# A gated cross-attention and quantised feed-forward block on one core: work at the edges of its stages rearranged

## What is computed

```python
x = x + tanh(g_xattn) * attention(layernorm(x), ctx)   # x: 4 x 512 x 1024, ctx: 4 x 64 x 1024
x = x + tanh(g_ffn)   * ffn(layernorm(x))

# attention: 32 query heads and 8 key/value heads of 128, rotary angles, causal mask
queries, keys, values = rope(h @ Wq.T), rope(ctx @ Wk.T), ctx @ Wv.T
attn = softmax(where(causal, queries @ keys.T * 128**-0.5, min))   # 64 keys
out = (attn @ values) @ Wd.T

# ffn, 1024 -> 512 -> 1024, rows and weights rounded to whole numbers up to 127
gate, up = quant(h * inv_gate) @ w_gate.T, quant(h * inv_up) @ w_up.T   # scaled back
inter = clip(silu(gate) * up, -10, 10)
out = quant(inter * inv_inter) @ w_down.T
```

## Time and profile before

| | |
|---|---|
| median of three executions | 1485.55 us |
| the profiled execution | 1490.73 us |
| its span, first to last instruction | 1488.9 us |
| TensorE, VectorE, ScalarE, GpSimd busy | 1431.8, 1005.5, 563.2, 614.7 us |
| mean granted clock of TensorE | 0.993 |
| key and value stage, up to the first queries | about 64 us |
| half 0, half 1 of the attention | to about 711 us, to about 1351 us |
| feed-forward loop | about 1351 us to the end |

### The profile page before, as it was taken

The page is one execution under the profiler, slowest core; times in us unless marked ns, Lnnn a source line. Parts: engine busy times, 40 slices in busy tenths (PEclk is TensorE's granted clock), DMA queues, the critical chain, the costliest instruction groups (busy, mean ns, idle before and its releaser), DMA issues.

```text
span 1488.9 us, 19163 instructions
## 1 busy us (share of the span) xinstructions
PE 1431.8 (96%) x7248; PEld 1169.9 (79%) x7248; DVE 1005.5 (68%) x1563; ACT 563.2 (38%) x864; POOL 614.7 (41%) x429
## 2 busy tenths in 40 slices
PE   7999999999999999999999999999999999997887
PEld 7878888888888888887878888888888888874443
DVE  5866575757576766667475757566666666677997
ACT  4424141414242323244542423232322323147995
POOL 3435242434343343440343433434433434233784
PEclk9999999999999999999999999999999999998999
DMA  8834343433425243437265242433333334464565
GB/s 296 251 95 107 72 114 72 106 88 82 112 64 119 68 106 80 108 78 238 74 177 137 70 107 61 95 76 94 83 89 86 94 72 108 93 206 148 120 128 99
DMA packets 327131, 166.52 MB, mean 112 GB/s; under 512 B 275200, under 2 KB 290048, under 8 KB 326656
## 3 DMA queue, kind: packets, MB, share of 16 engines
q1 hardware_dynamic: 324448, 154.29, 39.0%
q0 software_dynamic: 2592, 11.01, 4.5%
HBM read 132.74 MB, written 35.65 MB: 113 GB/s over the span
## 4 chain that ended last, share of the span: by engine, by line
PE 79%; DVE 12%; ACT 3%; DMA 2%; issue 2%; POOL 2%; SPq 1%; ACTq 0%; POOLq 0%; DVEq 0%
PE psum L561 16%; PE psum L563 16%; PE psum L562 16%; PE psum L615 8%; PE psum L650 7%; PE psum L652 7%; PE psum L651 7%; DVE psum L1625 2%; DVE vw_lo L1354 1%; DVE res L1672 1%; DMA acc<-in_x 1%; DMA wv_raw<-in_wv_t 1%; DVE xg L1635 1%; POOL rot L1239 1%; DVE pt_lo L1354 1%
## 5 line engine op out<-in xcount | busy, mean ns | idle before, releaser
L561 PE MATMUL psum<-xt_hi,wq_hi 128*128 128x512 f32 x1024 | 402.1, 393 | 2.6 <-DVE xt_lo L1354 2.6
L562 PE MATMUL psum<-xt_lo,wq_hi 128*128 128x512 f32 x1024 | 399.7, 390 | 0.0
L563 PE MATMUL psum<-xt_hi,wq_lo 128*128 128x512 f32 x1024 | 399.7, 390 | 0.0
L1211 POOL TENSOR_TENSOR wq_lo<-wq_raw,wq_hi 128x512 fp32r<-128x512 f32 x128 | 170.0, 1340 | 490.7 <-ACT wq_hi L918 490.7
L1515 DVE TENSOR_TENSOR acc<-psum,acc 128x512 f32<-128x512 f32 x224 | 151.3, 681 | 140.3 <-PE psum L652 140.3
L1239 POOL TENSOR_TENSOR rot<-rot 128x1024 f32<-128x1024 f32 x64 | 153.5, 2399 | 207.8 <-DVE rot L1458 207.0
L561 PEld LDWEIGHTS psum<-xt_hi,wq_hi 128*128 128x128 f32 x1024 | 193.1, 189 | 42.2 <-DVE xt_lo L1354 2.8
L563 PEld LDWEIGHTS psum<-xt_hi,wq_lo 128*128 128x128 f32 x1024 | 192.9, 188 | 40.8
L964 ACT ACTIVATE vw_hi<-psum 64x512 fp32r<-64x512 f32 x256 | 151.4, 591 | 194.0 <-PE psum L563 190.3
L562 PEld LDWEIGHTS psum<-xt_lo,wq_hi 128*128 128x128 f32 x1024 | 192.9, 188 | 39.5
L1354 DVE TENSOR_TENSOR vw_lo<-psum,vw_hi 64x512 fp32r<-64x512 f32 x256 | 175.4, 686 | 52.9 <-ACT vw_hi L964 46.8
(11 more groups left out here) (151 smaller groups left out, 1915.8 us busy)
## 6 DMA issues: line engine op xcount, KB each, us to landing
wq_raw<-in_wq_t SPq DMA_DIRECT2D x128, 256.0 KB, 4.4
wd_raw<-in_wd_t SPq DMA_DIRECT2D x128, 256.0 KB, 3.6
p_scratch<-prob SPq DMA_DIRECT2D x60, 256.0 KB, 2.0
pt_raw<-p_scratch SPq DMA_DIRECT2D x240, 64.0 KB, 2.5
acc<-in_x SPq DMA_DIRECT2D x16, 512.0 KB, 5.5
out_x<-acc SPq DMA_DIRECT2D x16, 512.0 KB, 3.9
xa<-out_x SPq DMA_DIRECT2D x16, 512.0 KB, 3.6
out_x<-res POOLq DMA_DIRECT2D x15, 512.0 KB, 5.5
```

The lines of the kernel that those rows point to most:

```text
L561: pe.matmul(dst, a_hi, b_hi, start=start, stop=False)
L562: pe.matmul(dst, a_hi, b_lo, start=False, stop=False)
L563: return pe.matmul(dst, a_lo, b_hi, start=False, stop=stop)
L1211: pool.tensor_tensor(dst, full, hi.bitcast(F32), ALU.subtract).then_inc(done, 1)
```

## The change

**The start.** The statistics of tiles 6 and 7 move from VectorE to ScalarE (`late_statistics`: a Copy with a running sum, then a Square with one, and two small scalings). On VectorE the low parts of rows 2 and 3 move ahead of the statistics of tile 5, and `key_rows(7)` moves ahead of the normalisation of tiles 4 to 7. TensorE transposes tile 4 one query part later (half 0 only).

**The first group of each half.** `values(gg, 2)` moves from between parts 6 and 7 of unit 2 to behind part 1 of unit 3, with its copies on ScalarE and VectorE.

**The end of each half.** The subtraction of the softmax (`softmax_less`) moves behind `add(2)`, and its last multiplication (`softmax_c`) behind `add(3)`. Elsewhere the two new functions directly follow the steps that they are cut from.

**The feed-forward loop.** The root of tiles 8 to 11 is taken at step 2 and that of tiles 12 to 15 at step 8 (before: one root for 8 to 15, at step 4). The four `deviations` of tiles 12 to 15, two at step 2 and two at step 3 before, come one each at steps 4 to 7. The scaling of `v_sd` moves from ScalarE to GpSimd, ahead of its loop.

```diff
 # tensor, slot(): first group
-                    else:
+                    elif half:
                         turn_rows(half, 4)
                     queries(unit, 4)
                     if not filled:
+                        if half == 0:
+                            turn_rows(half, 4)
                         turn_rows(half, 5)
...
                     queries(unit, 6)
-                    values(gg, 1 if filled else 2)
+                    if filled:
+                        values(gg, 1)
                     queries(unit, 7)
                 if kind == 3 and not filled:
-                    for part in range(1, 4):
-                        queries(unit, part)
+                    queries(unit, 1)
+                    values(gg, 2)
+                    queries(unit, 2)
+                    queries(unit, 3)
 # scalar
+            def late_statistics():
+                last, junk = slice(HTILES - 2, HTILES), bank(O_BANK, 2)
+                act.wait_ge(xt_lo_done, 2)
+                for t in (HTILES - 2, HTILES - 1):
+                    act.wait_ge(x_in[t], 16)
+                    if t == HTILES - 1:
+                        act.wait_ge(late_done, 1)
+                    act.activation(junk, acc[:, t, :], ACT.Copy, accum_out=mv[:, t, 0:1]).then_inc(late_done, 1)
+                act.wait_ge(late_done, 2)
+                act.activation(mv[:, last, 0], mv[:, last, 0], ACT.Copy, scale=1.0 / DIM).then_inc(late_done, 1)
+                for t in (HTILES - 2, HTILES - 1):
+                    act.wait_ge(late_done, 3 + t - HTILES + 2)
+                    act.activation(junk, acc[:, t, :], ACT.Square, scale=-1.0, bias=mv[:, t, 0:1], accum_out=mv[:, t, 1:2]).then_inc(late_done, 1)
+                act.wait_ge(late_done, 5)
+                act.activation(mv[:, last, 1], mv[:, last, 1], ACT.Copy, scale=1.0 / DIM).then_inc(stat_done, 2)
...
-                if n == HTILES:
-                    act.wait_ge(norm2_done, 2)
+                if n in (HTILES, HTILES + BT):
+                    act.wait_ge(norm2_done, n // BT)
...
             copy_rows(0, 3)
+            late_statistics()
             root(HTILES, slice(BT, HTILES))
...
                 if s == 2:
-                    down_columns()
-                if s < 4:
-                    deviations(1, 2 * s)
-                    deviations(1, 2 * s + 1)
-                if s == 4:
-                    root(TILES + 2, slice(HTILES, TILES))
+                    root(TILES + 2, slice(HTILES, HTILES + BT))
+                if BT <= s < HTILES:
+                    deviations(1, s)
+                if s == HTILES:
+                    root(TILES + 3, slice(HTILES + BT, TILES))
 # gpsimd
             pool.wait_ge(fv_in, 32)
+            pool.tensor_scalar(v_sd[:, :], v_sd[:, :], gates[:, 1:2], 1.0, ALU.mult, ALU.mult).then_inc(vd_done, 1)
 # vector, last_outputs()
                 softmax_a(unit - 1)
                 add(gg - 1, 2)
+                softmax_less(unit - 1)
                 softmax_b(unit - 1)
                 add(gg - 1, 3)
+                softmax_c(unit - 1)
 # vector, the loop of the feed-forward
-                if s == 4:
-                    variances(slice(HTILES, TILES), TILES)
-                if s == 5:
-                    second_norm(5, 1)
+                if s == 1:
+                    variances(slice(HTILES, HTILES + BT), HTILES + BT)
+                if s == 3:
+                    second_norm(5, slice(HTILES, HTILES + BT))
+                if s == HTILES:
+                    variances(slice(HTILES + BT, TILES), TILES)
+                if s == HTILES + 1:
+                    second_norm(6, slice(HTILES + BT, TILES))
```

More of the change, by code:

```diff
@@ L1423, in reciprocal_root, with second_norm @@
                 dve.wait_ge(small_done, small)
-            def second_norm(n, half):
-                tiles = slice(half * HTILES, (half + 1) * HTILES)
+            def second_norm(n, tiles):
                 reciprocal_root(n, tiles, rstd2)
@@ L1469, in softmax_a, with softmax_less @@
                 dve.tensor_reduce(red[:, 0, :], view, AX_X, ALU.max).then_inc(max_done, 1)
+            def softmax_less(unit):
+                view = scores.rearrange("p (s k) -> p s k", k=KEYS)
                 dve.wait_ge(max_done, unit + 1)
@@ L1485, in softmax_b, with softmax_c @@
                 dve.tensor_scalar(top[:, 2, :], top[:, 2, :], gates[:, 0:1], None, ALU.mult).then_inc(share_done, 1)
+            def softmax_c(unit):
+                top = rows_of_softmax(unit)
                 dve.wait_ge(share_done, unit + 1)
@@ L1591, in slot @@
                         lower_probs(unit - 2)
-                    else:
-                        lower_values(gg, 2)
                 if kind == 3 and not filled:
                     turn_second(unit - 1)
+                    lower_values(gg, 2)
                     softmax_a(unit - 1)
+                    softmax_less(unit - 1)
                     lower_probs(unit - 2)
@@ L1620, in slot @@
                 if half == 1 and u == UPG + 1:
-                    second_norm(4, 0)
+                    second_norm(4, slice(0, HTILES))
             def greatest(top, src, done):
@@ L1782, in _ @@
             row_statistics(4)
+            lower_rows(0, 2)
+            lower_rows(0, 3)
             row_statistics(5)
             key_rows(6)
-            lower_rows(0, 2)
-            lower_rows(0, 3)
-            row_statistics(6)
-            row_statistics(7)
-            aggregate(slice(BT, HTILES), HTILES)
-            reciprocal_root(2, slice(BT, HTILES), rstd1)
-            normalise(4)
-            normalise(5)
-            normalise(6)
-            normalise(7)
-            key_rows(7)
+            key_rows(7)
+            aggregate(slice(BT, HTILES - 2), HTILES - 2)
+            reciprocal_root(2, slice(BT, HTILES), rstd1)
+            for t in range(BT, HTILES):
+                normalise(t)
             dve.wait_ge(cst_in, 32)
```

14 lines of the change are left out of this document (6 added, 8 removed).

## The result

The changed kernel takes 1491.06 us in the median of 20 executions (1486.85 to 1493.03), the kernel before 1486.53 (20 executions beside it, 1483.41 to 1490.83). The ratio is 1.0028, 95% interval 1.002 to 1.0036: slower by 4.2 us (3.0 to 5.4; 4.5 by the two medians), where 6.5 faster was forecast. The profiled executions hide most of it: 1491.20 us after with a span of 1489.4, 1490.73 before with 1488.9.

What follows compares the result with a forecast made beforehand. TensorE was taken to bound the attention, VectorE the feed-forward loop. Start -2.2, value block -3.7 and -2.0, additions +1.05 and loop +0.4 gave -6.45, from the median 1485.55 to 1479.1 us; range 1474.5 to 1482.0.

Steps and rivals of the forecast that it cites:

- What bounds the kernel: In both attention halves TensorE runs back to back, so a wait removed there is time gained one for one.
- The start, forecast -2.2: Start: queries begin without the 2.6 us wait and 1.5 us fall; a new 1.65 us wait for tile 4; gain 2.2 us.
- The four tiles take 2.98 us, to 72.6: Start: VectorE's normalisations of tiles 4 to 7 keep their earlier length of 2.98 us and end at 72.6.
- normalisation starts 67.9 + 1.86 - 0.2: Start: keys of block 7 done at 67.9, shorter aggregation after them, so VectorE's first normalisation starts at 69.55.
- The value block, forecast -3.7 and -2.0: First group of each half: value stall of 2.09 us goes; half 0 gains 3.7 us including a clock fall, half 1 2.0.
- The limit in half 1: Value block, half 1: GpSimd's query turn behind the wq roundings holds the score to 757.9; gain 2.0 of a possible 2.7.
- The additions, forecast +1.05: End of each half: the multiplication delays the sixth output 0.65 us, half 1's fifth output is 0.4 late; 1.05 us slower.
- The loop, forecast +0.4: Feed-forward loop: next step 1.0 us earlier, then steps 4 to 9 take 47.95 against 46.53; net 0.4 us slower.
- The next step starts 2.2 - 1.2 = 1.0 earlier, 1.2 being `second_norm`: Loop, step 3: `qi` comes 2.2 us earlier, `second_norm` there takes 1.2, so step 4 starts 1.0 us earlier.
- The fall at the new stall: Rival, start: the clock falls behind the new wait at tile 4, costing 1.3 to 1.5 us, giving 1480.5; chance 0.2.
- The clock did fall ahead of `down(0)`: Loop: the forecast kept the lower clock at `down(0)`; a rival, chance 0.12, had no fall, -3 us, 1476.1.
- The slower case: Rival, loop: ScalarE late in steps 5 to 9, lower clock stays, steps about 4 us longer, 1487.5; chance 0.03.

Runs made afterwards that it cites:

- the one with the keys behind: New start, but the keys of block 7 put back behind the four normalisations; on the kernel before with the new start alone, 1485.53 us (0.9986).
- the mended four: Changed loop with second_norm(5) ahead of the dequantisation of gate in step 3; on the kernel before with the loop's part alone, 1486.29 us (1.0).
- start_wd_held: Kernel before with the new start alone, GpSimd held from rounding wd until the normalisations are done; 1485.49 us (0.9992).
- after_norm_early: The changed kernel with second_norm(5) alone moved ahead of the dequantisation in step 3; 1485.13 us (0.9987).
- the parts' single ratios: Kernel before with one part of the change alone: value block 0.9971, start 1.0032, additions 1.0024, loop 1.0036.
- before_again: A second trace of the kernel before, nothing changed; 1487.02 us, span 1485.1.
- start_keys_behind: Kernel before with the new start alone, but the keys of block 7 behind the four normalisations as before; 1485.53 us (0.9986).
- adds_product_held: Kernel before with the additions' part alone, GpSimd's first product with v_iu held until the last softmax multiplication is done; 1488.93 us (1.0012).

## Why the prediction was wrong

The sizes below are means over the traces that share a part, so that one execution's loads don't decide. The old start has seven (first score at 85.98 us), the changed one four (87.79), the one with the keys behind six (83.54). The old loop has nine traces (turn_gate(0) to turn_gate(15) 120.75 us), the changed four (124.74), the mended four (119.80).

**What bounds the kernel** held: a wait of TensorE removed in the attention is gained in full, and 561.6 to 561.8 us between third and last score of half 0 are the same in every kernel.

**The start, forecast -2.2, measured +1.8.** The step that failed is "The four tiles take 2.98 us, to 72.6" and, ahead of it, "normalisation starts 67.9 + 1.86 - 0.2". I took VectorE's durations from rows in which GpSimd stood idle, and moved the work to where it rounds wd; that it does so is due to the same move, since `key_rows(7)` ahead of the normalisations lets GpSimd go on to wd earlier: at 68.02, 1.3 us ahead of the first normalisation, where in before it began at 75.49, 6.8 us behind it. The four tiles took 4.84 us, tile 4 alone 1.71 in place of 0.81, and the two products ahead 0.50 and 1.19 in place of 0.16 each, so tile 4 was 2.3 us late. That the normalisations began at 69.35, close to the 69.55 of the sum, was luck: from the statistics of tile 4 on they took 13.4 us where 12.0 was summed, and that stretch happened to begin 1.6 us earlier. The other part is the clock. In all four traces with the changed start TensorE waits 2.72 to 3.13 us at tile 4 and the clock falls behind it; in start_wd_held it waits 1.60, about the 1.65 of the forecast, and the clock stays at 1.00. A fall costs some 1.2 us (next paragraph). The gain was oversized as well: the stall that goes is 2.60 us in the trace of before, but 1.97 in the mean of the seven old starts (1.22 to 2.69), and two of them have no fall behind it. The rest stood: queries at 61.4 with no wait, the bare wait for GpSimd's addition (1.50 for my 1.26), ScalarE's late statistics hidden (ready at 64.5). One reading was off as well: the last transposition of before is put at 77.47 + 0.82, where the earlier trace rows has 1.06; 78.29 is where the next matmul starts, a row that they lack. With the keys behind, the start gains 2.4.

**The value block, forecast -3.7 and -2.0, measured -4.0 and -1.8** (28.34 in the mean of the nine traces with the new place, 30.15 in eight of the nine with the old one, the ninth having a fall of the clock there). Right in mechanism, and in size with some luck. The part of the clock in it is confirmed: three traces with the old place have no fall at that stall (30.14 to the third score in place of 31.4), so a fall costs 1.2 us, not 1.5, and without one the gain is 2.7, not the 2.24 summed; the two errors nearly cancel. The limit in half 1, GpSimd's turn behind the roundings of wq, is the 1.19 us that score still waits, at 754.91.

**The additions, forecast +1.05, measured +0.4 and +1.8.** The terms for the order alone were right in sign and too large (0.6 us in all, once GpSimd is held). The failed step is the duration of the multiplication, which the sum leaves at its 0.65 us of delay: it took 2.45 us, 1.76 more. What I left out is that the multiplication, moved 0.6 us later, falls behind the start of GpSimd's product. In the trace of before (VectorE's row, then GpSimd's) the multiplication was first, by 0.23 us:

```profile
1330.05 0.69 DVE L1487 TENSOR_TENSOR prob<-prob,red 128x512 f32<-128x512 f32 x1
...
1330.28 4.59 POOL L1306 TENSOR_TENSOR xu<-yb,v_iu 128x1024 f32<-128x1024 bf16 x2 [5.60 <-ACT yb L1067]
```

**The loop, forecast +0.4, measured +4.0.** The step that failed is "The next step starts 2.2 - 1.2 = 1.0 earlier, 1.2 being `second_norm`". It took 3.5 us, from 1373.14 to the next reduction at 1376.65. That alone is 2.3. The first reduction of step 4 comes 33.41 us behind turn_gate(0) in the mean of the four traces, 31.94 in the nine old ones: 1.5 later, where 1.0 earlier was forecast. Behind it step 5 lasts 9.76 us, where 7.9 was summed, since `down(2)` fell to the lower clock: 1.9. Step 6, at 7.23 in place of 7.8, gives 0.6 of it back, so that steps 4 to 9 take 49.2 us where 47.95 was summed. The rest was as summed: `qi` 2.2 earlier, steps of 7.82 and 7.84 us with a deviation, 9.32 for step 9. The table loads cost 1.3 us each (the one at 1362.91 is followed by its root at 1364.20), and the 2.8 us more that a drain behind them would have added did not come. That the two go together is shown by one mend removing both: turn_gate(15) comes 4.1 us earlier in after_norm_early than in after, 4.9 by the means, steps 4 to 9 take 47.75 us, nearly the 47.95, and no fall stands in step 5 of any of the four mended loops. Whether the clock would have fallen without the two waits of 1.5 us was not tried by itself.

The corrected sum is +1.8 - 4.0 - 1.8 + 2.2 + 4.0 = +2.2, against 4.2 (3.0 to 5.4 by the interval). The 2 us between are within what the start and the middle of half 1 scatter, and stay unplaced. So does the difference between the whole, 4.2, and the parts' single ratios, which times 1486.6 sum to -4.3 + 4.8 + 3.6 + 5.4 = +9.5. The root of their squared half intervals is 3.6, less than that difference; but all four ratios are to the same 14 executions of before, whose error is counted four times, so 3.6 is too small a bound.

**The rivals.** The fall at the new stall came in all four traces, as its 0.2 allowed, but behind a stall made longer by GpSimd; behind one of the length forecast it did not come. The clock did fall ahead of `down(0)`, in every trace. The slower case had its mechanism nearly right, a longer pause and the lower clock in a step of the loop, but I priced it from the second step and gave it 0.03, for want of a reason why `xg` should be late. With that reason, one such step came in all four traces with the changed loop.

## What to carry to other kernels

A duration from a row holds only with the neighbour that it had there. When VectorE work is moved, look up GpSimd's rows at the new place, and when a move lets GpSimd run earlier, look at what VectorE does then: an operation with both inputs in SBUF, or one like the normalisation, can cost the rest of GpSimd's instruction, here over seven times its own length. Such an operation is safe where the other engine waits for it anyway: `second_norm` there cost nothing and made the loop 4.9 us shorter by the means. And one trace is one execution: cut it into stages and compare stages over several kernels that share them.

## Unexpected of the hardware

VectorE's products of 0.16 to 0.22 us took up to 1.25 us, each ending within 0.04 us of GpSimd's instruction. Its longer ones ended 0.55 us behind it: the multiplication of 0.69 us, 2.45 here, at 1329.95 where GpSimd's first product ended at 1329.40, and the two normalisations of 0.81, 1.71 and 1.76 here, likewise. An addition with an input in PSUM (0.68) and a reduction (1.22) kept their time.

GpSimd paid too where VectorE was there first or was already waiting. Three roundings of wd took 4.17 us beside the normalisations and 3.77 in start_wd_held, the third alone 1.72 in place of 1.27. Its first product with `v_iu` takes 2.47 us in each trace where the multiplication starts 0.23 us ahead of it, and 2.15 where it starts first.

The same 2.09 us stall of TensorE in half 0 had a fall of the clock behind it in before, before_again and four other traces, and none in three (start_wd_held, start_keys_behind, adds_product_held). Its twin in half 1 had none in eight of nine; the ninth is adds_product_held, where the clock was at 0.50 from 751.6 us to 755.0 (31.45 us to the third score in place of 30.14).
